# The last output block of an adapter and LoRA kernel, stored in two halves of its partitions from two queues

## The reference

```python
y = einsum('bij,bkj->bik', x, weight[adapter_ids])         # adapter, 512 x 512
q = y[:, 107:-1, :].mean(axis=1)
routing = softmax(q @ router_W.T + router_b)               # 8 experts
base = y @ W.T + b
t = einsum('bsd,erd->bser', y, A)                          # rank 16
lora = einsum('bser,eor,be->bso', t, B, routing) * 2
out = x + base + lora
```

## Time and profile before

| | |
|---|---|
| Time, median of 3 runs | 74.7 us (74.18, 74.70, 76.09) |
| Time of the profiled execution | 74.49 us |
| Span of the profiled execution, first to last instruction | 72.8 us |
| TensorE busy | 67.7 us (93%) |
| VectorE busy | 38.5 us (53%) |
| ScalarE busy | 26.4 us (36%) |
| Bytes moved by DMA | 15.30 MB |
| Granted TensorE clock, mean | 0.995 of 2.4 GHz |

### The profile page before, as it was taken

The page is one execution under the profiler, slowest core; times in us unless marked ns, Lnnn a source line. Parts: engine busy times, 40 slices in busy tenths (PEclk is TensorE's granted clock), DMA queues, the critical chain, the costliest instruction groups (busy, mean ns, idle before and its releaser), DMA issues.

```text
span 72.8 us, 1123 instructions
## 1 busy us (share of the span) xinstructions
PE 67.7 (93%) x404; PEld 52.8 (73%) x404; DVE 38.5 (53%) x99; ACT 26.4 (36%) x56; POOL 1.2 (2%) x10
## 2 busy tenths in 40 slices
PE   3997999998999999999999999999999999999930
PEld 1332244543698479998998899989789999999920
DVE  1000000225838945999974599699936098341620
ACT  0061003338258835993026997300060320240000
POOL 6000000000000000000000000000000000000000
PEclk9999999999999999999999999999999999999997
DMA  0828999999999999999724013105241320610142
GB/s 0 286 63 275 376 374 405 344 409 421 423 412 405 408 412 405 412 408 365 320 52 108 5 43 70 40 0 212 92 104 29 83 66 0 245 52 0 59 158 72
DMA packets 6774, 15.30 MB, mean 210 GB/s; under 512 B 752, under 2 KB 3312, under 8 KB 6768
## 3 DMA queue, kind: packets, MB, share of 16 engines
q1 hardware_dynamic: 6192, 14.31, 52.6%
q10 hardware_dynamic: 576, 0.92, 4.2%
HBM read 12.08 MB, written 2.10 MB: 195 GB/s over the span
## 4 chain that ended last, share of the span: by engine, by line
PE 72%; DMA 13%; SPq 9%; issue 1%; DVE 1%
PE ps_o L514 31%; DMA wc_raw<-in_wcT_dram 13%; PE ps_o L531 8%; PE ps_t L514 8%; PE ps_y L485 7%; SPq L164 4%; SPq L169 3%; PE ps_yT L496 3%; PE ps_yT L498 3%; PE ps_yT L497 3%; PE ps_y L496 3%; PE ps_y L497 3%; PE ps_y L498 2%; PE ps_yT L507 1%; SPq L189 1%
## 5 line engine op out<-in xcount | busy, mean ns | idle before, releaser
L514 PE MATMUL ps_o<-yT_hi,az_hi 128*128 128x256 f32 x64 | 18.5, 289 | 0.0
L514 PE MATMUL ps_o<-yT_hi,az_lo 128*128 128x256 f32 x64 | 17.9, 279 | 0.0
L514 PE MATMUL ps_o<-yT_lo,az_hi 128*128 128x256 f32 x64 | 17.9, 279 | 0.0
L485 PE MATMUL ps_y<-wc_raw,xT_raw 128*128 128x512 f32 x24 | 11.8, 611 | 0.8 <-DMA wc_raw<-in_wcT_dram 0.7
L514 PEld LDWEIGHTS ps_o<-yT_hi,az_hi 128*128 128x128 f32 x64 | 12.0, 188 | 0.3 <-issue 0.2
L514 PEld LDWEIGHTS ps_o<-yT_hi,az_lo 128*128 128x128 f32 x64 | 12.0, 188 | 0.3 <-issue 0.2
L514 PEld LDWEIGHTS ps_o<-yT_lo,az_hi 128*128 128x128 f32 x64 | 12.0, 188 | 0.0
L367 DVE TENSOR_TENSOR yT_lo<-ps_yT,yT_hi 128x512 fp32r<-128x512 f32 x4 | 2.7, 686 | 15.2 <-ACT yT_hi L267 15.2
L360 DVE TENSOR_TENSOR wc_lo<-wc_raw,wc_hi 128x1024 fp32r<-128x1024 f32 x8 | 9.5, 1209 | 0.0
L485 PEld LDWEIGHTS ps_y<-wc_raw,xT_raw 128*128 128x128 f32 x24 | 4.0, 191 | 7.1 <-issue 4.4
L418 DVE SCALAR_TENSOR_TENSOR o_sb<-ps_o,rest_raw,xT_raw 128x256 f32<-128x256 f32 x16 | 7.1, 477 | 3.5 <-PE ps_o L531 3.5
(11 more groups left out here) (61 smaller groups left out, 101.4 us busy)
## 6 DMA issues: line engine op xcount, KB each, us to landing
wc_raw<-in_wcT_dram SPq DMA_DIRECT2D x15, 512.0 KB, 13.9
xT_raw<-in_xT_dram SPq DMA_DIRECT2D x3, 512.0 KB, 13.4
out_dram<-o_sb SPq DMA_DIRECT2D x3, 512.0 KB, 3.3
rest_raw<-in_rest_dram SPq DMA_DIRECT2D x2, 512.0 KB, 10.8
yT_raw<-y_turn SPq DMA_DIRECT2D x14, 64.0 KB, 2.2
rest_raw<-in_rest_dram SPq DMA_DIRECT2D x1, 534.0 KB, 9.1
xT_raw<-in_xT_dram ACTq DMA_DIRECT2D x1, 512.0 KB, 3.3
out_dram<-o_sb SPq DMA_DIRECT2D x4, 128.0 KB, 1.9
```

What stands on the lines that cost most here:

```text
L485: last = mm(bank[:], xT_raw[:, b, c, :], wc_raw[:, b, c, :], start=(c == 0), stop=(c == C - 1))
L514: last = mm(bank[:, 0:N2], stat[:, n, c, :], mov[pair][:, c].rearrange("p b s -> p (b s)"), start=(c == 0 and k == 0), stop=(stop and c == ...
```

## The change

The four stores of the last pair were all issued by SP. Now SP stores chunks 0 to 2 as before, and chunk 3 is stored by two DMAs of 64 rows x 1 KB each: partitions 0 to 63 from SP and partitions 64 to 127 from ACT. Both wait for `o_ready[3]` to reach 4. The second half has a semaphore of its own, for which SP waits at the end.

```diff
-        last_stored = [sem(f"last_stored{c}") for c in range(C)]
+        last_stored = [sem(f"last_stored{c}") for c in range(C + 1)]
...
+        def store_last(queue, half):
+            rows = slice(half * P // 2, (half + 1) * P // 2)
+            queue.wait_ge(o_ready[C - 1], PAIRS)
+            queue.dma_start(out[PAIRS - 1, rows, C - 1], o_sb[rows, PAIRS - 1, C - 1].rearrange("p b s -> p (b s)"))\
+                .then_inc(last_stored[C - 1 + half], 16)
...
         @block.sync
...
             store(PAIRS - 2)
-            for c in range(C):
+            for c in range(C - 1):
                 sp.wait_ge(o_ready[c], PAIRS)
                 sp.dma_start(out[PAIRS - 1, :, c], o_sb[:, PAIRS - 1, c].rearrange("p b s -> p (b s)"))\
                     .then_inc(last_stored[c], 16)
+            store_last(sp, 0)
             for g in range(PAIRS - 1):
                 sp.wait_ge(stored[g], 16)
-            for c in range(C):
+            for c in range(C + 1):
                 sp.wait_ge(last_stored[c], 16)
...
         @block.scalar
...
             exponent(PAIRS - 1)
             hi_tsT(PAIRS - 1)
+            store_last(act, 1)
```

## The result

The changed kernel takes 75.14 us in the median of 17 runs, against 74.70 us for 17 runs of the kernel before. The ratio is 1.008, with a 95% interval of 1.0058 to 1.0103: slower by 0.6 us, clear of the measurement's noise, and well inside 2%.

A forecast was written before the change was run, and what follows sets the result against it. TensorE's matmuls and first weight loads bound nearly all the span; the change touches only the last 2.45 us. Terms 0 + 0 + 0 + 0.1 + 0 made 74.49 into 74.6, or 74.7 us as a median; range 73.9 to 75.7 us.

The forecast's parts named there:

- slower rival: ACT's DMA between issue and landing: the second queue's half is served late, 0.3 to 0.6 us slower, 75.1 us; chance 0.22.
- sign of being wrong: Last stretch: ACT's half landing after 2.3 us or later, both within 1.6 us, or time moving ahead of 70.35 us.
- SP's issue: SP's issue of the last store, 0.33 us before: nothing gained, or at most 0.17 us; taken as no gain.
- second half's lateness: ACT's half landing later than SP's at the end: nothing, or 0.4 us lost; taken as 0.1 us.
- pair at 55.95: Earlier 64 KB moves of yT_raw by SP and ACT together: issues 544 and 637 ns, landings after 2.1 and 2.5 us.
- The packets: The last store's 0.54 us of packets on the DMA engines: nothing, or 0.27 us gained; taken as nothing.
- ACT's wait: ACT's new wait and issue for the second half: entered 5.2 us before VectorE frees it, so no cost.
- SP's eighth semaphore: One more final wait on SP, for ACT's half: no more than 0.1 us, taken as nothing.
- side-by-side rival: Last store's issue, first-packet wait and packets: halves run in parallel, 0.15 to 0.7 us faster, 74.2 us; chance 0.18.
- rule of the Trainium skill: Transfers to disjoint partition halves: "Don't bother", both spread over all 16 DMA engines; read as a sum of 0, 74.5 us.

## Why the prediction was wrong

Forecast were 0.1 us more and 74.7 us; it became 0.6 us more by the ratio, 0.45 us in the stretch itself. The sign was right, the size was not: some five times the 0.1 us. The median of 75.14 us lies in the range and beside the slower rival's 75.1 us, but that rival had a chance of 0.22, and its mechanism, ACT's half served late, is only part of what happened; that the number fits is in part luck. The prediction's own sign of being wrong, ACT's half landing after 2.3 us or later, did show (2.4 us). Two terms failed: SP's issue, which was put at nothing with no loss allowed for, and the second half's lateness, which was taken at 0.1 us and measured 0.4 us.

**The first step that failed is SP's issue.** It was bounded with "nothing gained, or half of 0.33", as a cost that fewer rows could only lower, and the reading was that "the issue looks like a fixed cost". In the runs a 64-row issue takes 0.22 us longer, and its first packet comes 0.39 us later, on SP and ACT alike and without a partner. The bound left out the loss without a reason that excludes one. The trace did hold a hint: the 64 KB moves of SP took 542 ns at the least, against 332 ns at the least for the plain 128-row stores. In the pair at 55.95 the first packet comes 1.20 us after the issue, too. I read 544 against 637 ns within the pair and not 544 against 332 ns across the two kinds. Whether those moves are dear for the same reason was not tested; they read 32 partitions and write 128, so it isn't the number 64 that they share with the stores.

**The packets** were taken as no change, with a bound of 0.27 us gained. They took 0.20 us more, since ACT's half comes in 0.3 us behind SP's, and 64 rows alone need 0.45 us for half the bytes. The shorter wait behind the last packet, 0.14 us less, was not foreseen and takes some of that back. The forecast that one half wouldn't make the other's transfer shorter held.

**The second half's lateness** had the right sign and place, and its upper bound was right: the partner costs ACT's half 0.4 us in landing (2.4 against 2.0 us alone), just the 0.4 us of the pair in the earlier trace rows. I took 0.1 us of it, for the issue's length and because of the other shape and the second moves. The first reason was wrong: ACT's issue is only 0.03 us longer than SP's in the changed kernel (578 against 551 ns), and where ACT issued first it was SP's half that came late, so the lateness belongs to the second of two stores and not to ACT.

**ACT's wait and SP's eighth semaphore** cost nothing, as said: ACT's issue was over at 71.0, and SP's last wait for a store ends at 72.8 with the landing, followed by the branch at 72.9. VectorE's last block ended 0.05 us later than before; ahead of it the chain was up to 0.15 us behind in between (its longest run of matmuls starts at 62.87 and not at 62.72), for no reason that the change gives. The packets were 80 and 80.

**The side-by-side rival** is refuted: the issue doesn't get shorter with fewer rows, and even one half alone with nothing else to do lands 0.1 us later than the whole. The rule of the Trainium skill quoted in the prediction ("DMA: Bandwidth & Descriptors", section "Rules for kernel authors") was right to say "Don't bother", but the zero that I made of it was too kind. The halves don't cost the same as the whole; here they cost 0.45 us.

How much of the loss is whose depends on what is taken away first. With the partner gone (one half alone), 0.1 us of loss is left in the landing, so the partner is worth the rest, 0.3 to 0.4 us. With the shape gone and the partner kept, 0.1 us is left in the tail where each half has 128 partitions, and 0.25 us with 96 and 32 rows, so the shape is worth 0.2 to 0.4 us. Either step takes away half of the loss or more, and the two prices are not parts of one sum.

## What to carry to other kernels

Leave a final store in one piece of 128 partitions. If it must be cut, cut columns, since the first store of 64 rows costs 0.2 us more to issue and 0.4 us more to start than any of the other row counts tried here. A second queue helped only where the two transfers could start apart, by a quarter of a microsecond here; two stores released at the same moment delay the later one by 0.1 to 0.6 us, and in some pairs the earlier one too. And when a bound is drawn from rows of one shape, look for rows of any other shape before excluding one side.

## What was not expected of the hardware

The issue time of a store on SP isn't monotonic in its rows: 314 to 360 ns for 16, 32, 48, 80, 96, 112 and 128 rows, but 551 ns for the first store of 64 rows on an engine, 510 ns for the second, 466 to 473 ns from the third on. From the third on it doesn't depend on bytes (64 rows x 512 bytes, 1 KB and 4 KB), and the second takes 510 ns for partitions 0 to 63 as for 64 to 127. Nothing in these runs says why. The rate of the packets, on the other hand, has no such exception: 123 GB/s for 48 rows, 146 for 64, 178 for 80 and 243 to 252 for 128, so smaller stores simply move slower.
